# Scan, tile order, loads and weight rounding in the first stage of an LRU-attention and int8-FFN kernel

## The reference

```python
def xattn(q, k, v):                      # k = v = ctx
    r_t = 0.9 * r_(t-1) + k_t * v_t      # a scan over time, r_0 = k_0 * v_0
    return q * r
x = x + xattn(layernorm(x), ctx, ctx)
h = relu(quant_linear(layernorm(x), w1, b1))
x = x + quant_linear(h, w2, b2)
# quant_linear: activations rounded to uint8 with ONE scale from the maximum over the whole tensor,
# weights to int8 with a scale per output row, bias to int32 units
```

## Time and profile before

| | before |
|---|---|
| median of 3 runs | 1264.55 us (1264.29 to 1264.74) |
| the profiled execution's own time | 1265.31 us |
| its span | 1263.5 us |
| TensorE / VectorE / ScalarE / GpSimd busy | 96% / 69% / 78% / 13% |
| last VectorE statistics of stage one end | 317.8 us |
| first matmul of stage two (L833) | 329.2 us |
| first matmul of stage three (L875) | 810.0 us |
| mean DMA rate | 355 GB/s |

### The profile page before, as it was taken

One profiled execution on the slowest core, in us unless ns is written; L12 is line 12 of the kernel. 1 busy time (PEld: TensorE's weight loads), 2 busy tenths in 40 slices (PEclk: granted clock), 3 DMA queues, 4 the chain that ended last, 5 costly groups with the idle time before them and its releaser, 6 DMA issues.

```text
span 1263.5 us, 15533 instructions
## 1 busy us (share of the span) xinstructions
PE 1213.5 (96%) x5386; PEld 562.1 (44%) x5386; DVE 872.2 (69%) x1262; ACT 979.9 (78%) x1211; POOL 162.3 (13%) x394
## 2 busy tenths in 40 slices
PE   5998999999699999999999999799999999999997
PEld 2444444444344444444444444344444444444443
DVE  4887999886577777777777777566545655654554
ACT  4788999887577777777777776688887888888776
POOL 2646556444000000000000000000000000000000
PEclk9999999999799999999999999899999999999999
DMA  9999999972277799999999998699999999999998
GB/s 354 403 406 333 389 363 341 346 277 81 118 321 289 305 394 407 359 365 362 362 358 351 348 363 317 229 334 419 418 417 417 417 418 417 417 418 416 416 417 325
DMA packets 134614, 448.78 MB, mean 355 GB/s; under 512 B 10740, under 2 KB 10760, under 8 KB 123400
## 3 DMA queue, kind: packets, MB, share of 16 engines
q1 hardware_dynamic: 94744, 331.40, 66.2%
q10 hardware_dynamic: 39792, 116.40, 25.8%
HBM read 254.81 MB, written 192.94 MB: 354 GB/s over the span
## 4 chain that ended last, share of the span: by engine, by line
PE 80%; POOL 6%; issue 5%; DVE 4%; DMA 3%; ACT 2%; SPq 1%; ACTq 0%; POOLq 0%; DVEq 0%
PE ps L833 35%; PE ps L875 33%; PE ps L811 9%; PE ps L855 2%; DMA xq<-hidden_scratch 2%; POOL xq L444 2%; DVE st L644 1%; DVE st L630 1%; DVE xq L639 1%; DMA xq<-in_x_dram 1%; POOL rstd L436 1%; POOL cs_bc L428 1%; ACT xq L478 1%; ACT xq L589 0%; SPq L317 0%
## 5 line engine op out<-in xcount | busy, mean ns | idle before, releaser
L875 PE MATMUL ps<-w2T,xq 128*128 128x512 f16 x2048 | 446.4, 381 | 4.2 <-ACT xq L589 3.8
L833 PE MATMUL ps<-xq,w1T 128*128 128x512 f16 x2048 | 448.7, 380 | 1.4 <-DVE xq L710 1.4
L589 ACT ACTIVATE xq<-xq,hb,hs 128x512 f16<-128x512 f32 x494 | 357.3, 801 | 83.6 <-PE ps L875 57.5
L701 DVE TENSOR_REDUCE work<-xq 128x2 f32<-128x1024 f32 x255 | 311.0, 1220 | 125.9 <-ACT xq L534 125.9
L534 ACT ACTIVATE xq<-ps 128x1024 f32<-128x1024 f32 x255 | 260.9, 1023 | 123.1 <-PE ps L833 122.9
L875 PEld LDWEIGHTS ps<-w2T,xq 128*128 128x128 f16 x2048 | 200.0, 98 | 250.6 <-ACT xq L589 9.8
L811 PE MATMUL ps<-xq,work 128*128 128x512 f32 x640 | 283.0, 603 | 24.7 <-ACT xq L468 24.7
L833 PEld LDWEIGHTS ps<-xq,w1T 128*128 128x128 f16 x2048 | 199.1, 98 | 237.0 <-issue 1.9
L749 DVE TENSOR_TENSOR work<-ps,cs_bc 128x512 f32<-128x512 f32 x128 | 88.4, 691 | 185.0 <-PE ps L875 178.6
L811 PEld LDWEIGHTS ps<-xq,work 128*128 128x128 f32 x640 | 122.9, 193 | 178.0 <-issue 161.0
L478 ACT ACTIVATE xq<-ps,ones,cs_bc 128x512 f32<-128x512 f32 x128 | 98.9, 772 | 24.8 <-PE ps L811 23.8
(11 more groups left out here) (99 smaller groups left out, 444.9 us busy)
## 6 DMA issues: line engine op xcount, KB each, us to landing
hidden_scratch<-xq SPq DMA_DIRECT2D x240, 512.0 KB, 6.0
xq<-hidden_scratch SPq DMA_DIRECT2D x232, 512.0 KB, 21.2
work<-x_scratch ACTq DMA_DIRECT2D x42, 1024.0 KB, 11.4
xq<-in_ctx_dram ACTq DMA_DIRECT2D x31, 1024.0 KB, 9.2
xq<-in_x_dram SPq DMA_DIRECT2D x24, 1024.0 KB, 12.0
x_scratch<-xq SPq DMA_DIRECT2D x24, 1024.0 KB, 8.4
out_dram<-work ACTq DMA_DIRECT2D x24, 1024.0 KB, 12.0
xq<-in_L_ffn_w_dram SPq DMA_DIRECT2D x8, 1024.0 KB, 7.8
```

Source lines behind the costliest of these rows:

```text
L589: act.activation(hq[c % HQ], src[:, c % 2, :], ACT.Relu, bias=hb[:, q:q + 1], scale=hs[:, q:q + 1]).then_inc(h_scaled, 1)
L701: dve.tensor_reduce(hmax[:, b * NF + 2 * q:b * NF + 2 * q + 2], src, AX.X, ALU.max).then_inc(kept_maxed, 1)
L833: last = pe.matmul(bank, w1T[:, k, f * P:(f + 1) * P], xq_rows(b, k), start=(k == 0), stop=(k == KD - 1))
L875: last = pe.matmul(acc_bank(s, i), src[:, i * P:(i + 1) * P], w2T[:, q, :], start=first, stop=final)
```

## The change

- **Layout**: `x`, `ctx` and `out` are viewed `(p i)` and no longer `(i p)`: partition p holds times 4p to 4p + 3, contiguous in DRAM.
- **Scan**: row group 0 takes 4 matmuls (`scan_first`), and each further one adds a single matmul with a scaled identity (`own_mat`) to the same PSUM bank (`scan_next`), after ScalarE has read the bank. So 4 + 3 = 7 a batch, and one bank a batch. The powers of 0.9 that this leaves over are folded into 1/sigma by constants (`half_x`, `per_row_x`, `eps_x`).
- **Order**: the tiles of batches j and j + 1 are interleaved on all engines: (j+1, 0), (j, 2), (j+1, 1), (j, 3). The square runs three batches ahead, x statistics four (`XLEAD`), with rings of 8.
- **Loads**: ctx moves from ScalarE's queue to SyncE's, with 4 buffers; x is loaded 6 ahead; a batch's store is issued ahead of the loads, and `load_ctx(j+4)`, which waits for the last scan of batch j, closes each turn. The product has 4 single-tile buffers (`g1`) in place of 8.
- **Weights**: GpSimd multiplies by 1/scale and by 2^-24 and writes f16 itself; `int_weights` on ScalarE is gone. VectorE takes one of the two copies out of PSUM. The factor 2^24 that this leaves in each product is put back in `hs`, in `diag_cs` and in the maximum (L721, L728, L736).

```diff
-CS = 3
-RING = 4
+CS = 4
+RING = 8
+XLEAD = 4
-LEAD = 5
+LEAD = 6
...
-    y_groups = [[j, j + 1] for j in range(0, NB - 2, 2)] + [[NB - 2], [NB - 1]]
+    y_groups = [[j, j + 1] for j in range(0, NB - 2, 2)] + [[NB - 2, NB - 1]]
...
+    scans, tiles = [(0, 0)], []
+    for j in range(-1, NB):
+        scans += [t for t in ((j + 1, 1), (j, 3), (j + 1, 2), (j + 2, 0)) if 0 <= t[0] < NB]
+        tiles += [t for t in ((j + 1, 0), (j, 2), (j + 1, 1), (j, 3)) if 0 <= t[0] < NB]
+    scan_at = {t: n for n, t in enumerate(scans)}
+    tile_at = {t: n for n, t in enumerate(tiles)}
...
-    x_rows = x.rearrange("b (i p) d -> b p i d", p=P)
-    ctx_rows = ctx_in.rearrange("b (i p) d -> b p i d", p=P)
-    out_rows = out.rearrange("b (i p) d -> b p i d", p=P)
+    x_rows = x.rearrange("b (p i) d -> b p i d", p=P)
+    ctx_rows = ctx_in.rearrange("b (p i) d -> b p i d", p=P)
+    out_rows = out.rearrange("b (p i) d -> b p i d", p=P)
...
-        g1 = [arena[:, n * ROW:(n + 1) * ROW].rearrange("p (i d) -> p i d", i=NI) for n in range(2)]
-        ct = [arena[:, (2 + n) * ROW:(3 + n) * ROW].rearrange("p (i d) -> p i d", i=NI) for n in range(CS)]
+        g1 = [arena[:, n * D:(n + 1) * D] for n in range(NI)]
+        ct = [arena[:, (1 + n) * ROW:(2 + n) * ROW].rearrange("p (i d) -> p i d", i=NI) for n in range(CS)]
...
-                sp.wait_ge(x2_done, (b + 1) * NI)
+                sp.wait_ge(x2_done, tile_at[(b, NI - 1)] + 1)
                 sp.dma_start(x2_dram[b], xt[b % XS].rearrange("p i d -> p (i d)")).then_inc(x2_stored[b % XS], 16)
-            sp.dma_start(ct[0], ctx_rows[0]).then_inc(ctx_loaded[0], 16)
-            for j in range(LEAD):
-                load_x(j)
-                if j == 2:
-                    load_weights(0)
-                    sp.dma_start(brow[:, :], b1_rows).then_inc(b_loaded, 16)
-                    sp.dma_start(brow2[:, :], b2_rows).then_inc(b_loaded, 16)
+            def load_ctx(j):
+                if j >= CS:
+                    sp.wait_ge(scan_ready, scan_at[(j - CS, NI - 1)] + 1)
+                sp.dma_start(ct[j % CS], ctx_rows[j]).then_inc(ctx_loaded[j % CS], 16)
+            load_ctx(0)
+            load_x(0)
+            load_x(1)
+            for j in range(1, CS):
+                load_ctx(j)
+                load_x(j + 1)
+            load_weights(0)
+            sp.dma_start(brow[:, :], b1_rows).then_inc(b_loaded, 16)
+            sp.dma_start(brow2[:, :], b2_rows).then_inc(b_loaded, 16)
+            load_x(CS + 1)
             for j in range(NB):
+                if j > 0 and j - 1 not in late:
+                    store_x2(j - 1)
                 if j + LEAD < NB:
                     load_x(j + LEAD)
                 for m in weights_at(j + 2):
                     if m > 0:
                         load_weights(m)
-                if j > 0 and j - 1 not in late:
-                    store_x2(j - 1)
+                if j + CS < NB:
+                    load_ctx(j + CS)
+            if NB - 1 not in late:
+                store_x2(NB - 1)
...
+            gp.memset(decays, DECAY ** NI)
+            for i in range(NI):
+                gp.memset(half_x.rearrange("p (n i) -> p n i", i=NI)[:, :, i], 0.5 * DECAY ** -i)
+                gp.memset(per_row_x.rearrange("p (n i) -> p n i", i=NI)[:, :, i], DECAY ** (-2 * i) / D)
+                gp.memset(eps_x.rearrange("p (n i) -> p n i", i=NI)[:, :, i], LN_EPS * DECAY ** (-2 * i))
...
+            for i in range(NI):
+                part = impulse[:, i * P:(i + 1) * P]
+                gp.affine_select(out=part, in_=part, compare_op=ALU.not_equal, fill=DECAY ** (NI - i) if i else 1.0, base=1 if i else 0,
+                                 pattern=[[-1, P]], channel_multiplier=1)
...
-                gp.tensor_tensor(t[3], t[1], per_row[:, 0:n], ALU.mult)
-                step(gp.tensor_tensor(t[4], t[2], half[:, 0:n], ALU.mult))
-                gp.tensor_tensor(t[5], t[3], eps[:, 0:n], ALU.add)
+                gp.tensor_tensor(t[3], t[1], per[:, 0:n], ALU.mult)
+                step(gp.tensor_tensor(t[4], t[2], halves[:, 0:n], ALU.mult))
+                gp.tensor_tensor(t[5], t[3], floor[:, 0:n], ALU.add)
...
                 rows = (4, 1)[w]
+                wait_count(gp, w_turned, 2 * (m - 1))
                 for c in range(rows):
-                    row = w_stage[m % 2].rearrange("p (c d) -> p c d", c=rows)[:, c, :]
-                    last = gp.tensor_scalar(row, row, isw[w][:, k * rows + c:k * rows + c + 1], ROUND_ANY, ALU.mult, ALU.add)
-                last.then_inc(w_rounded, 1)
+                    part = slice(c * ROW // rows, (c + 1) * ROW // rows)
+                    last = gp.tensor_scalar(w_ints[m % 2][:, part], w_stage[m % 2][:, part], isw[w][:, k * rows + c:k * rows + c + 1],
+                                            UNIT, ALU.mult, ALU.mult)
+                last.then_inc(w_int, 1)
             x_stats(x_group[0])
             x_stats(x_group[1])
-            for j in range(NB):
-                if j % 2 == 1 and j + 1 < NB:
-                    x_stats(x_group[j + 1])
-                if j % 2 == 0 and j >= 2:
-                    y_stats(y_group[j - 1])
+            x_stats(x_group[2])
+            for j in range(NB - 2):
+                if j % 2 == 1:
+                    if j + XLEAD < NB:
+                        x_stats(x_group[j + XLEAD])
+                    y_stats(y_group[j])
                 for m in weights_at(j):
                     round_weights(m)
-            y_stats(y_group[NB - 2])
             y_stats(y_group[NB - 1])
...
-            def load_ctx(j):
-                wait_count(act, scan_ready, (j - CS + 1) * NI)
-                act.dma_start(ct[j % CS], ctx_rows[j]).then_inc(ctx_loaded[j % CS], 16)
             def factors(j, i):
                 u = j * NI + i
+                n = tile_at[(j, i)]
                 if i == 0:
                     act.wait_ge(stats1_ready, x_group[j] + 1)
                 xi = xt[j % XS][:, i, :]
                 act.activation(xi, xi, ACT.Identity, bias=nmean1[:, u:u + 1])
-                act.wait_ge(scan_ready, u + 1)
-                wait_count(act, x2_done, u + 1 - 2 * NI)
-                act.activation(g1[j % 2][:, i, :], scan_bank(j, i), ACT.Identity, bias=ones[:, 0:1],
+                act.wait_ge(scan_ready, scan_at[(j, i)] + 1)
+                wait_count(act, x2_done, n + 1 - len(g1))
+                act.activation(g1[n % len(g1)], scan_bank(j), ACT.Identity, bias=ones[:, 0:1],
                                scale=rstd1[:, u:u + 1]).then_inc(scan_scaled, 1)
-            def int_weights(m):
-                act.wait_ge(w_rounded, m + 1)
-                wait_count(act, w_turned, 2 * (m - 1))
-                act.activation(w_ints[m % 2], w_stage[m % 2], ACT.Identity, bias=minus_round[:, 0:1]).then_inc(w_int, 1)
-
...
+                act.wait_ge(w_turned, 2 * m + 1)
+                into, turned = turned_weights(m, 0)
+                act.activation(into, turned, ACT.Copy).then_inc(w_kept, 1)
...
-            load_ctx(1)
-            load_ctx(2)
             square(0)
+            factors(0, 0)
+            square(1)
+            factors(0, 1)
+            square(2)
             for j in range(NB):
-                factors(j, 0)
-                factors(j, 1)
                 if j + 1 < NB:
-                    square(j + 1)
+                    factors(j + 1, 0)
                 factors(j, 2)
+                if j + 1 < NB:
+                    factors(j + 1, 1)
                 factors(j, 3)
-                if j + CS < NB:
-                    load_ctx(j + CS)
-                for m in weights_at(j - 1):
-                    int_weights(m)
+                if j + 3 < NB:
+                    square(j + 3)
                 for m in weights_at(j - 3):
                     keep_weights(m)
...
+            for i in range(1, NI):
+                link(dve.tensor_scalar(own_mat[:, (i - 1) * P:i * P], ident[:, :], DECAY ** -i, None, ALU.mult))
...
+            def keep_weights(m):
+                dve.wait_ge(w_turned, 2 * m + 2)
+                into, turned = turned_weights(m, 1)
+                dve.tensor_copy(into, turned).then_inc(w_kept, 1)
...
+            x_stats_of(0)
+            x_stats_of(1)
+            product(0)
+            product(1)
+            y_stats(0)
+            x_stats_of(2)
+            x_stats_of(3)
+            for n in range(2, NU):
+                j, i = divmod(n - 2, NI)
+                product(n)
+                y_stats(n - 1)
+                if j < NB - 1:
+                    x_stats(j + XLEAD, i)
+                if i == NI - 1:
+                    for m in weights_at(j):
+                        weight_scales(m)
+                    for m in weights_at(j - 3):
+                        keep_weights(m)
+            y_stats(NU - 1)
+            for m in weights_at(NB - 1):
+                weight_scales(m)
...
```

(81 more changed lines are left out.)

47 lines of the change are left out of this document (19 added, 28 removed).

## The result

The changed kernel takes 1235.03 us (1232.85 to 1235.45, 4 runs) against 1264.43 for the kernel before: 0.9764 of its time, 95% interval 0.9747 to 0.9781. In a second comparison the unaltered changed kernel gave 0.9764 again (0.975 to 0.9777). Forecast: 1231.4, range 1222 to 1252.

The account below looks back on a forecast made before the run. TensorE's scan was taken as the bound from 210 us, waits for VectorE's scales as part of the weight batches; after the change, VectorE. 317.8 - (281 + 3) - 0.7 = 33 us; 1265.3 - 33.1 - 0.8 = 1231.4 us, range 1222 to 1252.

Parts of the forecast that it names:

- Stage one's end: VectorE's passes and waits put stage one's last statistics at 281 us plus 3 for stalls, before 317.8.
- the product that overlaps a w2 quarter: VectorE's product during GpSimd's w2 pass: 1.85 us where 0.69 is usual, four times, 4.6 us kept.
- The start: Stage one's opening: x statistics of batch 4 wait for loads until 27 us, with 19 VectorE passes done.
- The end: Stage one's last 14 tiles: VectorE waits for TensorE at 1.5 us a tile, 4 us more.
- the stalls: Stage one's waits for late x and ctx loads: 3 us added, bounds 0 and 12.
- DMA: Stage one's loads at 408 GB/s: last x lands at 246 us, stage end 274, 7 us from VectorE's limit.
- Rival A: Stage one's DMA runs at only 357 GB/s, the stage ends at 304 us, kernel 1252 us; chance 0.13.
- Rival B: ScalarE and TensorE wait for each other over the scan's PSUM bank, 0.5 us each time: 1248 us; chance 0.13.
- Rival C: TensorE, idling in pieces, loses clock; at 1.2 GHz throughout, the kernel is slower at 1342 us; chance 0.04.
- Rival D: GpSimd's f16 weight write takes over three times the present pass; at five times 1293 us; chance 0.03.
- the removed 24 us: ScalarE's dropped weight pass and copy in stage one: worth little alone, ScalarE at 232 us against VectorE's 261.
- Stage three: Its work is kept and output stores change layout: taken as 0, with at most 4 us to be won.

Follow-up runs that it names:

- e9: Changed kernel with VectorE's second statistics pass over 128 of the 512 features; 1231.56 us against 1266.45 for the kernel before.
- e6: Changed kernel with the first matmul of each batch's scan issued twice, 8 matmuls a batch; 0.9774 of the kernel before.
- e4: Kernel before, with only GpSimd writing the f16 weights itself and ScalarE's pass over them gone; 1266.23 against 1265.37 us, ratio 1.0011.
- e1: Changed kernel with ScalarE's pass over the rounded weights put back, GpSimd rounding in f32 again; 0.9828 of the kernel before.
- ctx before x: Changed kernel with SyncE's turn reordered to store, ctx load, then x one batch further ahead; 0.9739 of the kernel before, once more 0.9744.
- e11: The kernel with ctx before x, with ScalarE's pass over the rounded weights put back; 0.9784 of the kernel before the change.

## Why the prediction was right, and where it was not

- **Stage one's end** was forecast from VectorE's passes at 281 + 3 for waits, and came at 282.6. Its terms hold: work 262.6 us in all (the sum had 384 x 0.60 + 26 + 4.6 = 261) and 19.9 us of idle time (the sum had 23), copy 0.67. One was high: the product that overlaps a w2 quarter on GpSimd takes 1.25 us, not 1.85, four times, 2.4 us less. But the sum has VectorE as the only bound, and `e9` shows that it was not: with 44 us less of VectorE's work the stage was only 3 to 6 us shorter. That the bounds lay so close together is part of why it came out right.
- **The start** was put at 27 us with 19 passes done, which is 15.6 us idle; VectorE was idle 12 to 14 us in the first 30. The end was put at 4 us of waits and the stalls at 3; after 210 us VectorE waited 4.8, between 30 and 210 us 3.0.
- **DMA** at 408 GB/s was forecast to end the stage at 274 alone; with VectorE relieved, the stage's statistics end at 278.5 (`e9`), 4 to 6 us before those of the changed kernel. That a next limit lay a few us behind is shown; that it is DMA's bytes is not, since the chain there is the ctx loop. The last x was issued at 238.5 us and such loads landed after 8 to 10, so near 248 (246 forecast). Two readings of the earlier trace rows were loose: DMA's share was 0.95 to 0.98 in three windows between 90 and 210 us, and the 0.39 belongs to 270 to 300 us.
- **Rival A** is out: 403 to 419 GB/s in most windows where it needed 357. What the Trainium skill says (DMA: Bandwidth & Descriptors, Where 436 GB/s comes from) of about 358 GB/s on the HBM side for a core does not hold here, with one core busy.
- **Rival B** took 14.8 us of ScalarE's waiting for TensorE, 0.15 us a step over 96 steps and not 0.5. Nearly all of VectorE's waits after 30 us were for ScalarE's product factor, 7.8 us in all; how much of that came from the scan is not shown.
- **Rival C** half happened: granted clock 0.86 to 0.94 in most windows. A higher clock and one more matmul together changed nothing measurable (`e6`). At 7 matmuls TensorE was busy 22.8 to 28.0 of 30 us in the windows from 30 to 240.
- **Rival D** is out: f16 costs GpSimd what f32 did.
- **The step that failed**, though the total came out right, is ScalarE's: "the removed 24 us is worth little alone, because VectorE and DMA cover it". Taken alone on the old schedule it is so, for another reason (`e4`). In the changed kernel 16 of them are worth 7 to 10 us of stage one (`e1`), and 8 with ctx before x (`e11`). I compared sums of work (232 against 261 us) and left out that ScalarE stands in a loop with TensorE and ctx. Its waits there are 21 us for ctx and 15 for the scan, and in the changed kernel none of its waits was for VectorE to free a product tile: it had no slack against VectorE. An estimate, 232 + 36 = 268 against VectorE's 263, shows the two level.
- **Stage three** was put at 0, with only a gain of up to 4 us allowed. It lost 3.8 us. The distance to the forecast is 3.6 (1235.0 against 1231.4): 3.8 of stage three, 0.4 of stage two and 0.8 between span and median, less the 1.4 by which stage one did better. A bound on one side was not justified: nothing in the rows excluded a loss when an access pattern changes.

## What to carry to other kernels

Work taken from an engine is worth what the engine's waits let through: the same 16 us were worth 0 where the engine stood behind another's program order, and 7 to 10 where it stood in a loop. Before calling an engine covered, add its waits on the loop to its work, and look whether it ever waits for the engine that is said to cover it. The sum is a warning and not a forecast, since the waits shift when the work does (`e11`). When one bound falls, the next ones may lie a few us behind, as here; then try the order of the loads: moving one `dma_start` within a queue's turn, with one batch more of lead for the other, gave 3 us.

## What the runs showed of the hardware

- Reads and writes together reached 419 to 426 GB/s over windows of 30 us of stage one with x and ctx in rows of 8 KB; with rows of 2 KB before, at most 402 and 408. No run separates the rows from the schedule there. In stage three, where of the DMA work only the output's view changed, windows of 30 us moved 417 before and 418 after. A single output store of 1 MB landed after 12.0 us (median) in rows of 2 KB and 8.0 in rows of 8 KB.
- GpSimd's two-operand pass costs the same into f16 and f32: 2386 and 2388 ns for 128x2048, and for 128x512 on one schedule 1035 ns both (`e4` and before), on the other 897 ns both (changed and `e1`). A product issued while it runs is held back: before, one starts at 133.82, 1.07 us into a pass that ends at 135.14, and takes 1.85 us; in the changed kernel (rows below) one starts at 124.47, 1.67 us into the pass, and takes 1.25; in `e9` one starts 1.27 into it and takes 1.65. All end 0.53 us after the pass does. `e4` writes f16 and has the 1.85 of before, `e1` writes f32 and has 1.25, so the stretch is set by how early in the pass the product comes and not by the output type. It goes the other way too: a 128x512 pass of GpSimd that starts while a product is running takes 1.09 and 1.15 us (at 105.13 and 106.87 us of the changed kernel), the passes between them 0.69. The Trainium skill (SBUF — State Buffer, Who interferes with whom) says that a VectorE instruction with two SBUF inputs contends with a GpSimd one that reads SBUF and that the later one waits; these rows agree.

```profile
122.80 2.39 POOL L481 TENSOR_SCALAR xq<-xq,isw 128x2048 f16<-128x2048 f32 x1 [1.67 <-DVE isw L647]
124.47 1.25 DVE L666 CUSTOM_DVE_ANT_0 xq<-xq 128x512 f32<-128x512 f32 x1
```

- With one f32 matmul more in each batch the granted clock of the windows from 30 to 180 us was 0.95 to 1.00, and without it 0.86 to 0.92 in one execution and 0.83 to 0.99 in another. The matmul's 27 us and the clock together did not show in the time.
